# The first norm of four batches moved into the first cross attention, and first work of four stages issued one stage early

## The chip, the cores and the metric

One core of a Trainium2 chip runs the whole program. The metric is the device time of one execution in microseconds (us). TensorE multiplies, VectorE (DVE), ScalarE (ACT) and GpSimd (POOL) do the rest, and SyncE (SP) starts the transfers. "PE" is TensorE in the rows below.

## The reference

`x` is 8 batches of 256 rows by 256 columns; `ctx` is 8 batches of 64 rows. Four sublayers follow each other, each on a layernorm of `x`:

```python
x = x + tanh(g_xattn[0]) * cross_attention_0(layernorm(x), ctx)   # 16 heads of 128, 4 key heads, norm of q and k
x = x + tanh(g_ffn[0])   * block_0(layernorm(x))                   # h = x + causal self attention(layernorm(x)); h + mixture of 4 experts(layernorm(h))
x = x + tanh(g_xattn[1]) * cross_attention_1(layernorm(x), ctx)   # rotary, keys = context keys and own causal keys
x = x + tanh(g_ffn[1])   * feed_forward_1(layernorm(x))            # silu(gate) * up, down, 704 wide
```

All is float32. Matmuls that need it are done as three matmuls of split values (high by high, low by high, high by low).

## The kernel before

The residual `R` stays on the chip for all 8 batches, and so do `XTh` and `XTl`, the transposed normalised input of the current stage in a high and a low part. The program is six stages one after the other: the opening `c0` (context keys and values, first norm of all 8 batches, splitting of the first weights), the first cross attention `x0`, the self attention `f0`, the experts `moe`, the second cross attention `x1`, and the feed forward `ff`. An attention stage has 32 steps: head group `g = i // 8`, batch `i % 8`. The experts have 32 steps too (batch `c // 4`, expert `c % 4`), and `ff` has 8 batches of 6 slices.

Within a stage each of the five engines has its own list of instructions, written out by hand in program order, and semaphores order them against each other. An engine works its list strictly in order: an instruction that waits holds back all behind it. At the end of a stage every engine drains, raises one semaphore `bar` (L117 in `phase_end`) and waits until all five have; POOL then clears the semaphores of the stage one by one (L121) before it goes on. Nothing of the next stage is issued before that: no transfer of its constants, no matmul.

The norm of a batch (`row_norm`) is a chain over four engines: `stats` on DVE (L174, L177), `inverse` on POOL (a small addition and a power, L182 and L184), `rows` on DVE (L189, both halves of the batch), `turn` on PE (four transposes, L197), then an ACT copy to `XTh` and a DVE subtraction to `XTl`.

In the opening these are ACT `high` (L413) and DVE `low` (L458), done for b = 0 to 7 in a loop; POOL's list has `norm.inverse(b)` and `weights(b)` (L145, L147) in turn, and SP's list has the eight weight transfers, each behind `split_done`, and behind them six small ones (L334 to L336), the last of which it awaits.

A step of `x0` is on DVE a softmax (`softmax`, L802 to L824) with `queries` for two steps ahead (L795); on ACT the exponential (L733), the copy of the transposed queries (`q_ev`, L717), `squares` (L728) and the copy of the transposed probabilities (L771); on POOL `low_w` and `norms` (L585, L588), which waits for `squares(i + 2, s, 1)`; on PE projections `proj(i + 2)` (L285 to L287), `q_tr` (L639), `scores` (L650), `p_tr` (L660), `out_proj` (L671), and every second step `vw` (into `pO`).

`f0` begins with seven transfers of constants (L923 to L928), then the projections 0 to 5 of step 0. Its queries and keys are rotated in chains: PE projection, ACT `swapped` (L1097), POOL three operations of 128x512 (L1388, L1391, L1394), DVE `take` (L1240). `moe` begins with the gates on DVE and ACT, with `up(0)` to `up(2)` on PE and ten transfers on SP, the spilled rows `moe_xs` (awaited by DVE in `bias(0)`, L2222) last but one. `x1` begins with the projections of step 0, their rotation and norm on DVE, ACT and POOL, and their transposes, before `scores(0, 0)` (L1532, L1534) and the first `soft` (L1784). Its end norms batches 6 and 7 after the last outputs are added. `ff` begins with three transfers of constants; ACT and DVE wait for all three (`const`, 48).

Of the kernel before, what the change touches and what calls it, by code (L numbers as in the profile page):

```python
# [24 lines left out]
P = 128  # L25
B, S, D = 8, 256, 256
SC = 64
# [41 lines left out]
def build(nc, d, out, spill, stop=99):  # L69
    ctx = ExitStack()  # L70
    with ctx:
# [89 lines left out]
        be1 = sb("be1", [P, E * D // P])  # L161
        before = sb("before", [P, E, E])

        def row_norm(name, scope, xn=None):
# [7 lines left out]
            def stats(e, b):  # L172
                for t in range(T):
                    e.bn_stats(bst[:, b % 2, t, :], R[:, T * b + t, :]).then_inc(s_bs, 1)  # L174
                e.wait_ge(s_bs, T * b + T)
# [4 lines left out]
            def inverse(e, b):  # L180
                e.wait_ge(s_st, b + 1)
                e.tensor_scalar(rstd[:, 0, b, :], mv[:, 0, b, :, 1], 1e-5, 1.0, ALU.add, ALU.mult).then_inc(s_p, 1)  # L182
                e.wait_ge(s_p, b + 1)
                e.tensor_tensor(rstd[:, 0, b, :], rstd[:, 0, b, :], mhalf[:, 0:T], ALU.pow).then_inc(s_rs, 1)  # L184

            def rows(e, b):
                e.wait_ge(s_rs, b + 1)
# [5 lines left out]
            def turn(e, b, bank):  # L193
                e.wait_ge(s_xn, b + 1)
# [103 lines left out]
        def first_stage(name, q, norm, cT, wkv, kb, sq, ss, KT, VT, bq, bk, bv, wcol, mask):  # L298
# [42 lines left out]
            def pe(e):  # L341
# [41 lines left out]
                for b in range(3, B):  # L383
                    norm_tr(b)
                phase_end(e, name)

            def act(e):
# [50 lines left out]
                for b in range(3, B):  # L438
                    high(b)
                phase_end(e, name)  # L440

            def dve(e):
# [27 lines left out]
                for b in range(B):  # L470
                    if b + 2 < B:
                        stats(b + 2)
                    low(b)
                    if b + 2 < B:
                        rows(b + 2)
                e.wait_ge(q["late"], 32)
# [3 lines left out]
            def pool(e):  # L480
# [24 lines left out]
            return Phase(sp, pool, act, dve, pe)  # L505

        x0 = ExitStack()

        def cross_attention_0():
# [36 lines left out]
            names = ("raw0", "raw1", "hi", "split", "proj", "qb", "sq", "rqa", "rq", "tr", "te",  # L546
# [6 lines left out]
            def sp(e):  # L553
                def body(i, s, nxt):
                    if nxt:
# [15 lines left out]
            def pool(e):  # L571
# [18 lines left out]
                def body(i, s, nxt):  # L590
# [21 lines left out]
            def pe(e):  # L612
                def proj(i, s, t):
                    e.wait_ge(q["split"], pos(i - 3))
                    slot = (i // 8) % 2
# [7 lines left out]
                def vw(i, hp):  # L623
# [55 lines left out]

                def body(i, s, nxt):  # L680
# [9 lines left out]
                    if i in (29, 31):  # L690
                        turn(i, i - 29)
                    if s == 0:
# [9 lines left out]
                    if not last:  # L702
                        scores(i + 1)
                    p_tr(i)
                    if i in (29, 31):
                        turn(i, i - 28)
                    if not first:
                        out_proj(i - 1, 1 - s)
                in_order(e, NI, body, 24)
# [1910 lines left out]
```

## Time and profile before

| | |
|---|---|
| median of 3 runs | 1831.43 us (1830.64 to 1831.76) |
| the profiled execution | 1833.69 us, span 1831.9 us |
| PE busy | 1717.3 us, 94% of the span |
| DVE, ACT, POOL busy | 61%, 72%, 58% |
| DMA | 40.69 MB, 22 GB/s |
| mean granted clock of PE | 0.975 |

The span is the time from the first to the last instruction of the profiled execution; the time of a run holds some 2 us more. In the page's 40 slices PE stands at 9 tenths nearly everywhere; the slices at the stage seams are the ones that don't: slice 1 (5), slice 8 (7 and 8 around 340 us) and slices 21, 24 and 37 to 39. The stages run from about 0 to 45.6 us (opening), to 335 (`x0`), to 953 (`f0`), to 1092 (`moe`), to 1711 (`x1`), and to the end (`ff`).

### The profile page before, as it was taken

To read this page: it belongs to the slowest core of one execution; us is meant where nothing else is said; L and a number is where in the kernel's file an instruction comes from. 1 tells how busy PE (TensorE), PEld (TensorE's weight loads), DVE (VectorE), ACT (ScalarE), POOL (GpSimd) and SP (SyncE) were. 2 spreads that over 40 slices of the span, in tenths; PEclk is the share of its full clock that TensorE was granted. 3 is DMA by queue.
4 is the path that set the end of the run, shared out by engine and by line. 5 is a ranking of instruction groups with operands and counts; after the bars stand their busy time and mean duration, and the time that the engine had idled before them with its cause. 6 is when DMAs were issued, how large, how long until landed. Compare 5 with 4: busy or idle time off the path is not lost.

```text
span 1831.9 us, 36545 instructions
## 1 busy us (share of the span) xinstructions
PE 1717.3 (94%) x11584; PEld 1559.8 (85%) x11584; DVE 1118.2 (61%) x3129; ACT 1327.2 (72%) x4300; POOL 1064.2 (58%) x1208
## 2 busy tenths in 40 slices
PE   5999999799999999999989978999999999998798
PEld 3788888588999999999977867888888888888797
DVE  5577778477766666666867774555555555565222
ACT  4677777588888888888855627888888888888211
POOL 4333337699989889899823115444444444454454
PEclk8999999899999999999989989999999999999899
DMA  4000001100000000000011100000000000000000
GB/s 135 18 16 18 16 30 53 53 19 13 18 19 19 18 19 13 19 13 19 13 59 43 29 18 5 12 9 12 9 12 9 12 9 18 14 21 8 9 19 24
DMA packets 29533, 40.69 MB, mean 22 GB/s; under 512 B 4896, under 2 KB 18464, under 8 KB 29216
## 3 DMA queue, kind: packets, MB, share of 16 engines
q1 hardware_dynamic: 29344, 38.35, 6.9%
q8 instruction: 97, 1.59, 0.4%
q14 instruction: 92, 0.75, 0.1%
HBM read 34.14 MB, written 4.19 MB: 21 GB/s over the span
## 4 chain that ended last, share of the span: by engine, by line
PE 65%; ACT 14%; issue 6%; POOL 5%; DVE 4%; DMA 1%; SPq 0%; POOLq 0%; ACTq 0%; DVEq 0%
PE pS L978 4%; PE pF L285 4%; ACT pA L1642 4%; PE pF L287 4%; PE pF L286 4%; PE pA L287 4%; PE pA L285 4%; PE pA L286 3%; PE pA L969 3%; PE pF L671 3%; PE pA L971 3%; PE pA L970 3%; PE pS L650 3%; PE pO L997 3%; ACT x_P L1668 3%
## 5 line engine op out<-in xcount | busy, mean ns | idle before, releaser
L285 PE MATMUL pA<-Wh,XTh 128*128 128x512 f32 (+1 forms) x512 | 221.8, 433 | 5.2 <-DVEq L117 2.9
L1388 POOL TENSOR_TENSOR f_sw<-f_sw,f_sin 128x512 f32<-128x512 f32 x128 | 181.4, 1417 | 44.2 <-ACT f_sw L1097 44.2
L287 PE MATMUL pA<-Wh,XTl 128*128 128x512 f32 (+1 forms) x512 | 189.0, 369 | 0.0
L286 PE MATMUL pA<-Wl,XTh 128*128 128x512 f32 (+1 forms) x512 | 188.0, 367 | 0.0
L1097 ACT ACTIVATE f_sw<-pA 64x512 f32<-64x512 f32 x256 | 151.7, 593 | 35.4 <-PE pA L971 31.5
L1391 POOL TENSOR_TENSOR f_sw<-f_sw,f_RB 128x512 f32<-128x512 f32 x128 | 169.2, 1322 | 10.0
L969 PE MATMUL pA<-XTh,Wh 128*128 128x256 f32 x512 | 163.4, 319 | 8.1 <-DMA wg<-in_w_gate 7.2
L1668 ACT ACTIVATE x_P<-x_P,x_nm 128x192 f32<-128x192 f32 (+1 forms) x256 | 127.9, 505 | 35.8 <-DVE x_nm L1784 35.8
L280 POOL TENSOR_TENSOR Wl<-RAW,Wh 128x256 fp32r<-128x256 f32 (+3 forms) x64 | 60.7, 949 | 155.3 <-ACT Wh L273 155.3
L970 PE MATMUL pA<-XTl,Wh 128*128 128x256 f32 x512 | 145.2, 284 | 0.0
L971 PE MATMUL pA<-XTh,Wl 128*128 128x256 f32 x512 | 145.2, 284 | 0.0
L1895 POOL TENSOR_TENSOR x_QR<-x_QR,x_t 128x512 f32<-128x512 f32 x64 | 82.3, 1286 | 99.9 <-DVE x_QR L1761 99.9
L1118 ACT ACTIVATE f_P<-f_P,f_nm 128x128 f32<-128x128 f32 (+1 forms) x256 | 114.0, 447 | 22.5 <-DVE f_nm L1257 22.2
L1676 ACT ACTIVATE x_P<-x_P,x_rs 128x192 f32<-128x192 f32 (+1 forms) x256 | 116.2, 507 | 7.2 <-DVE x_rs L1792 7.2
L285 PEld LDWEIGHTS pA<-Wh,XTh 128*128 128x128 f32 x512 | 97.9, 191 | 26.3 <-DVEq L117 3.7
L1784 DVE CUSTOM_DVE_ANT_0 x_P<-pS,x_mask,x_nrq 128x192 f32<-128x192 f32 (+1 forms) x256 | 113.3, 480 | 4.5 <-PE pS L1534 3.7
L286 PEld LDWEIGHTS pA<-Wl,XTh 128*128 128x128 f32 x512 | 98.0, 191 | 18.7
L287 PEld LDWEIGHTS pA<-Wh,XTl 128*128 128x128 f32 x512 | 97.5, 191 | 17.3
L978 PE MATMUL pS<-f_kT,f_qT 128*128 128x128 f32 (+1 forms) x512 | 106.2, 330 | 5.7 <-POOL f_kT L1394 5.7
L1257 DVE CUSTOM_DVE_ANT_0 f_P<-pS,f_mask 128x128 f32<-128x128 f32 (+1 forms) x256 | 80.8, 353 | 48.9 <-PE pS L978 47.9
L969 PEld LDWEIGHTS pA<-XTh,Wh 128*128 128x128 f32 x512 | 98.3, 192 | 11.4 <-issue 7.5
L1126 ACT ACTIVATE f_P<-f_P,f_rs 128x128 f32<-128x128 f32 (+1 forms) x256 | 101.6, 448 | 3.1 <-DVE f_rs L1265 3.0
(286 smaller groups left out, 6093.4 us busy)
## 6 DMA issues: line engine op xcount, KB each, us to landing
RAW<-in_w_f SPq DMA_DIRECT2D x32, 256.0 KB, 2.7
RAW<-in_w_x SPq DMA_DIRECT2D x32, 160.0 KB, 2.2
RAW<-in_w_x SPq DMA_DIRECT2D x32, 128.0 KB, 2.1
RAW<-in_w_ff SPq DMA_DIRECT2D x8, 288.0 KB, 2.7
R<-in_x SPq DMA_DIRECT2D x4, 512.0 KB, 7.2
x_spill<-R SPq DMA_DIRECT2D x8, 256.0 KB, 2.0
RAW<-in_w_moe SPq DMA_DIRECT2D x8, 256.0 KB, 2.6
moe_xs<-x_spill SPq DMA_DIRECT2D x8, 256.0 KB, 3.0
```

Source lines behind the costliest of these rows:

```text
L285: e.matmul(o, ah, bh, start=first, stop=False)
L286: e.matmul(o, ah, bl, start=False, stop=False)
L287: return e.matmul(o, al, bh, start=False, stop=last)
L969: e.matmul(o, Wh[g % 2][:, w], xh, start=(k == 0), stop=False)
L970: e.matmul(o, Wh[g % 2][:, w], xl, start=False, stop=False)
L971: ins = e.matmul(o, Wl[g % 2][:, w], xh, start=False, stop=(k == KD - 1))
L978: ins = e.matmul(pS[:, h % 2, OFF[t]:OFF[t] + WID[t]], qT[:, i % 2, h, t * P:(t + 1) * P], kT[:, i % 2, h, 0:WID[t]], start=True, stop=True)
L1097: ins = e.activation(sw[dst, n, :, :], pA[src, n % 2, :].rearrange("p (a n) -> p a n", a=2), ACT.Copy)
L1388: e.tensor_tensor(y, y, bc(sind[:, :], 1, 2), ALU.mult).then_inc(q["swm"], 1)
L1391: e.tensor_tensor(y, y, RB[:, g % 2, 2 * n:2 * n + 2, :], ALU.add).then_inc(q["swb"], 1)
L1668: ins = e.activation(x, x, ACT.Exp, scale=-1.0, bias=nm[:, h, t:t + 1], accum_out=sm[:, h, t:t + 1])
L1676: ins = e.activation(x, x, ACT.Copy, scale=rs[:, h, t:t + 1])
```

## The change

Six things change; what is computed stays the same.

1. Opening: `norm` is done for batches 0 to 3 only. POOL still splits all eight weight pieces.
2. `x0`, steps 0 to 3: the norm of batches 4 to 7 (`late`). In steps 0 and 2 two batches get `stats` and `rows` on DVE and `inverse` on POOL; in steps 1 and 3 they are turned into `pO`, copied by ACT and subtracted by DVE.
3. Seam `x0` to `f0`: `f0`'s constants are loaded in step 20 of `x0`; its projections 0 and 1 are done by PE in and after the last step.
4. Seam `f0` to `moe`: `up(0)` and `up(1)` (12 matmuls of 256 columns each) are done in the last step of `f0`.
5. Seam `moe` to `x1`: the head of `x1` up to the transposes of step 0 and the keys and values of step 1 is laid into and behind the last four steps of `moe`, on all engines. Some tiles of `moe` share memory with tiles of `x1`.
6. Seam `x1` to `ff`: `ff_gs` and `ff_us` are loaded in `x1`, the table of Silu is loaded at its end, the first two slices of `ff` are projected in its last step. The norm of batches 6 and 7 moves into the first two batches of `ff`.

```diff
@@ opening
-                for b in range(3, B):
-                    norm_tr(b)
+                norm_tr(3)
@@ opening, pool
-                for b in range(2, B):
-                    norm.inverse(e, b)
-                    weights(b)
+                for c in range(2, 8):
+                    if c < 4:
+                        norm.inverse(e, c)
+                    weights(c)
@@ x0, sp
+                    if i == 20:
+                        self_constants(e)
@@ x0, pool: body, behind norms(i + 2, s)
+                    if i in (0, 2):
+                        late.inverse(e, i + 4)
+                        late.inverse(e, i + 5)
@@ x0, pe
+                    if t == 0 and 4 <= i < B:
+                        e.wait_ge(q["llo"], i - 3)
...
+                    if i in (2, 4) and hp == 0:
+                        e.wait_ge(q["llo"], i)
...
+                    if i in (1, 3):
+                        late_turn(i, i + 3)
                     if s == 0:
                         vw(i, 0)
...
                     if not last:
                         scores(i + 1)
+                    else:
+                        next_proj(0)
                     p_tr(i)
...
+                    if i in (1, 3):
+                        late_turn(i, i + 4)
                     if not first:
                         out_proj(i - 1, 1 - s)
...
                 in_order(e, NI, body, 24)
+                next_proj(1)
                 out_proj(NI - 1, (NI - 1) % 2)
@@ x0, act: behind squares(i + 2, s, 0), and again behind squares(i + 2, s, 1) with i + 4
+                    if i in (1, 3):
+                        late_high(i + 3)
@@ x0, dve: softmax
                     if two_more:
                         queries(i + 2, s, 0)
+                    if i in (1, 3):
+                        late_low(i + 3)
                     e.wait_ge(q["ex"], i + 1)
@@ x0, dve: body
                     if two_more:
                         queries(i + 2, s, 1)
+                    if i in (0, 2):
+                        late.stats(e, i + 4)
+                        late.stats(e, i + 5)
+                        late_rows(i + 4)
+                        late_rows(i + 5)
+                    if i in (1, 3):
+                        late_low(i + 4)
@@ f0, pe: last step
                     if one:
                         proj(j, 4)
+                    else:
+                        next_up(0)
...
                     if one:
                         scores(j, 0)
+                    else:
+                        next_up(1)
@@ moe, pe: behind down(c)
+                    if c == NU - 4:
+                        e.wait_ge(q["split"], B)
+                        e.wait_ge(q["nlo"], 2)
+                        head.proj_kv(e, 0)
+                    if c == NU - 3:
+                        head.proj_q(e, 0, 0)
+                    if c == NU - 2:
+                        head.proj_q(e, 0, 1)
+                head.proj_kv(e, 1)
+                head.q_tr(e, 0, 0)
+                head.q_tr(e, 0, 1)
                 norm_tr(B - 1)
+                head.k_tr(e, 0)
@@ moe, dve
+                    if c == NU - 2:
+                        head.rotate_k(e, 0)
+                    if c == NU - 1:
+                        head.take_q(e, 0, 0)
...
                 norm_stats(B - 1)
+                head.take_q(e, 0, 1)
                 norm_rows(B - 1)
+                head.rotate_k(e, 1)
                 norm_low(B - 1)
@@ moe, pool
+                head.sum_q(e, 0, 0)
                 norm.inverse(e, B - 1)
+                head.sum_q(e, 0, 1)
+                head.inverse_norms_q(e, 0)
+                head.inverse_norm_k(e, 1)
+                head.sum_k(e, 1)
@@ x1, pe: last step, behind scores(i, 2), and next_up(e, 1) behind p_tr(i, 2)
+                    if not one:
+                        next_up(e, 0)
@@ x1, pe: end
                 out_proj(NI - 1, 0)
-                norm_tr(6)
                 out_proj(NI - 1, 1)
-                norm_tr(7)
@@ ff, dve
+                        if i == 0 and m == 1:
+                            scale_result()
+                        if i == 0 and m in (2, 3):
+                            norm.stats(e, 4 + m)
+                        if i == 0 and m in (4, 5):
+                            norm.rows(e, 2 + m)
```

## Rows read from the trace of the kernel before

**Rows 1.** The page, the chain that ended last: shares of the span by engine.

```profile
PE 65%; ACT 14%; issue 6%; POOL 5%; DVE 4%; DMA 1%; SPq 0%; POOLq 0%; ACTq 0%; DVEq 0%
```

**Rows 2.** Windows: length, busy time (x instructions) of PE, PEld, DVE, ACT, POOL, clock.

```profile
95.00:300.00 205.00, 204.23 (x1270) 181.99 (x1269) 160.51 (x287) 159.52 (x621) 82.79 (x116) 1.00 0.08 24
1716.00:1800.00 84.00, 80.27 (x663) 79.04 (x662) 21.26 (x43) 18.53 (x39) 48.53 (x81) 1.00 0.05 17
```

**Rows 3.** Timeline, end of the opening: start, length, instruction [idle before, releaser].

```profile
30.98 0.71 POOL L184 TENSOR_TENSOR rstd<-rstd,mhalf 128x2 f32<-128x2 f32 x1
31.80 1.20 DVE L189 TENSOR_SCALAR n_xn<-R,mv,rstd 128x256 f32<-128x256 f32 x2 [0.60 <-POOL rstd L184]
...
41.74 1.20 DVE L189 TENSOR_SCALAR n_xn<-R,mv,rstd 128x256 f32<-128x256 f32 x2 [0.59 <-POOL rstd L184]
...
45.63 0.79 PE L285 MATMUL pA<-Wh,XTh 128*128 128x512 f32 x1 [1.46 <-DVEq L117]
```

**Rows 4.** Timeline and DMA view, the opening's weights and last transfers.

```profile
21.48 15.04 SPq L136 DMA_DIRECT2D RAW<-in_w_x  x6
38.93 0.43 SPq L336 DMA_DIRECT2D before<-in_earlier  x1
...
before<-in_earlier SPq DMA_DIRECT2D x1, 8.0 KB, 2.6
...
28.80 0.73 POOL L147 TENSOR_TENSOR Wl<-RAW,Wh 128x256 fp32r<-128x256 f32 x1
```

**Rows 5.** Timeline of DVE, POOL and ACT, steps 0 to 3 of `x0`.

```profile
64.55 0.68 DVE L795 TENSOR_TENSOR x_qb<-pA,x_bq 128x512 f32<-128x512 f32 x1
66.69 0.69 DVE L802 TENSOR_TENSOR x_P<-pS,x_rq 128x512 f32<-128x512 f32 x1 [1.46 <-PE pS L660]
...
84.50 0.69 DVE L802 TENSOR_TENSOR x_P<-pS,x_rq 128x512 f32<-128x512 f32 x1 [1.58 <-PE pS L660]
...
68.86 1.66 POOL L588 TENSOR_TENSOR x_rq<-x_rq,mhalf 128x8 f32<-128x8 f32 x1
...
69.66 0.63 ACT L733 ACTIVATE x_P<-x_P 128x512 f32<-128x512 f32 x1 [0.91 <-DVE x_P L813]
70.20 1.07 ACT L717 ACTIVATE x_qT<-pT 128x512 f32<-128x512 f32 x2
```

**Rows 6.** The chain in order of time: squares, and `out_proj` at either clock.

```profile
282.33 1.27 ACT x_sq L728 x8
...
299.30 1.73 PE pF L671 x8
...
318.79 3.43 PE pF L671 x8
```

**Rows 7.** Timeline, end of `x0` and start of `f0`.

```profile
334.42 0.25 DVE L214 BATCH_NORM_AGGREGATE mv<-bst 128x2 f32<-128x6 f32 x2
...
339.98 0.55 PE L969 MATMUL pA<-XTh,Wh 128*128 128x256 f32 x1 [7.17 <-DMA wg<-in_w_gate]
...
344.26 1.27 POOL L1388 TENSOR_TENSOR f_sw<-f_sw,f_sin 128x512 f32<-128x512 f32 x1 [11.94 <-ACT f_sw L1097]
```

**Rows 8.** Timeline of DVE, start of `moe`.

```profile
965.07 1.35 DVE L2222 SCALAR_TENSOR_TENSOR moe_xs<-moe_b,moe_gcomb,moe_xs 128x256 f32<-128x256 f32 x2 [3.48 <-DMA moe_xs<-x_spill]
```

**Rows 9.** Timeline, end of `moe` and start of `x1`.

```profile
1091.22 0.69 DVE L2242 TENSOR_TENSOR XTl<-pF,XTh 128x512 fp32r<-128x512 f32 x1 [1.90 <-ACT XTh L2122]
...
1101.33 1.28 POOL L1895 TENSOR_TENSOR x_QR<-x_QR,x_t 128x512 f32<-128x512 f32 x1 [0.58 <-DVE x_QR L1761]
...
1107.41 0.41 DVE L1784 CUSTOM_DVE_ANT_0 x_P<-pS,x_mask,x_nrq 128x192 f32<-128x192 f32 x1
...
1117.41 0.70 PE L1552 MATMUL pO<-x_PT,x_V 128*128 128x256 f32 x2 [2.88 <-POOL x_VS L1872]
```

**Rows 10.** Timeline, end of `x1` and first slices of `ff`.

```profile
1710.08 1.26 POOL L1914 TENSOR_TENSOR XTl<-x_KT,XTh 128x512 fp32r<-128x512 f32 x1 [2.70 <-ACT XTh L1697]
...
1717.73 0.39 PE L2360 MATMUL pA<-XTh,Wh 128*128 128x256 f32 x1 [1.48 <-DVE ff_h L2413]
```

More of the change, by code:

```diff
@@ L437, in act @@
                 take_keys(3)
-                for b in range(3, B):
-                    high(b)
+                high(3)
                 phase_end(e, name)
@@ L796, in queries, with late_rows, late_low @@
                                     ).then_inc(q["qb"], 1)
+                def late_rows(b):
+                    e.wait_ge(q["ltr"], pos(b - 5))
+                    late.rows(e, b)
+                def late_low(b):
+                    e.wait_ge(q["lhi"], b - 3)
+                    e.tensor_tensor(XTl[:, :, columns(b)], pO[:, :].rearrange("p (k n) -> p k n", k=KD),
+                                    XTh[:, :, columns(b)].bitcast(F32), ALU.subtract).then_inc(q["llo"], 1)
                 def softmax(i, s, two_more):
@@ L1033, in pe, with next_up @@
                 e.wait_ge(q["const"], 96)
-                for n in range(NQ):
+                def next_up(c):
+                    e.wait_ge(q["taken"], NQ * NI)
+                    e.wait_ge(q["split"], NI - 6)
+                    e.wait_ge(q["nlo"], 1)
+                    experts_up(e, c)
+                for n in range(2, NQ):
                     proj(0, n)
@@ L1415, in cross_attention_1, with cross_head @@
+        Head = namedtuple("Head", "q QR qT kT V KR nrq at_p at_qk place proj_kv proj_q q_tr k_tr take_kv squares q_ev k_ev "
+                          "take_q rotate_k context_keys inverse_norm_k sum_k sum_q inverse_norms_q t2")
+        def cross_head(scope, KT, tables):
             cosT, sinT, cosk, sink = tables
             NU, NT = 3, 3
[L1417 to L1421 removed]
@@ L1474, in table, with proj_kv @@
                 return bc(halves(x[:, t, :]), 1, HG)
+            def proj_kv(e, i):
+                g = i // 8
+                if g:
+                    e.wait_ge(q["split"], 8 * (g - 1) + 5)
+                e.wait_ge(q["tq"], pos(T * (i - 1) + 1))
+                for t in range(T):
+                    for k in range(KD):
+                        cc = slice(WKV + k * 2 * HD, WKV + (k + 1) * 2 * HD)
+                        ins = three(e, pA[:, NU * i % 2, t * 2 * HD:(t + 1) * 2 * HD], x_part(XTh, i, k, t),
+                                    x_part(XTl, i, k, t), Wh[(g + 1) % 2][:, cc], Wl[(g + 1) % 2][:, cc],
+                                    k == 0, k == KD - 1)
+                ins.then_inc(q["proj"], 1)
@@ new lines, in proj_q @@
+            def proj_q(e, i, t):
+                g = i // 8
+                if g:
+                    e.wait_ge(q["split"], 8 * (g - 1) + 4)
+                if t == 0:
+                    e.wait_ge(q["tq"], T * i)
+                else:
+                    e.wait_ge(q["tk"], i + 1)
+                for k in range(KD):
+                    cc = slice(k * GW, (k + 1) * GW)
+                    ins = three(e, pA[:, (NU * i + 1 + t) % 2, :], x_part(XTh, i, k, t), x_part(XTl, i, k, t),
+                                Wh[(g + 1) % 2][:, cc], Wl[(g + 1) % 2][:, cc], k == 0, k == KD - 1)
+                ins.then_inc(q["proj"], 1)
@@ new lines, in take_kv, with squares @@
+            def take_kv(e, i):
+                e.wait_ge(q["proj"], NU * i + 1)
+                e.wait_ge(q["pv"], pos(HG * (i - 2)))
+                x = pA[:, NU * i % 2, :].rearrange("p (t a n) -> p t a n", t=T, a=2)
+                for t in range(T):
+                    e.activation(sk[:, t, :], x[:, t, 0, :], ACT.Square, accum_out=ssk[:, t:t + 1])
+                e.activation(V[:, i % 3, :, :], x[:, :, 1, :], ACT.Copy).then_inc(q["kv"], 1)
+            def squares(e, i, t):
+                e.wait_ge(q["rot"], T * i + t + 1)
+                e.wait_ge(q["rqa"], i)
+                for h in range(HG):
+                    x = pA[:, (NU * i + 1 + t) % 2, h * HD:(h + 1) * HD]
+                    ins = e.activation(x, x, ACT.Square, accum_out=ssq[:, t, h:h + 1])
+                ins.then_inc(q["tq"], 1)
@@ L1841, in dve @@
                     if two:
[L1842 removed]
+                        take_q(e, k, 0)
                     if one:
@@ L2435, in body @@
                                         ALU.subtract).then_inc(q["hl"], 1)
+                        if i == 0 and m in (3, 4):
+                            norm.inverse(e, 3 + m)
                         if m == 4 and not (i == 0):
```

623 lines of the change are left out of this document (315 added, 308 removed).

## The prediction

> **What bounds the kernel now.** I read first the chain of waits on the page: it runs through PE for 65% of the span [rows 1]. The windows come next: in `x0` from 95 to 300 us PE is busy 204.23 of 205 us at full clock, and in `ff` 80.27 of 84 us [rows 2]. So inside those stages only PE time counts, and time can come only from where PE is not fed. These places are the seams, and the timelines around them give the terms. The reader is to see there which engine starts last: at each seam something small (a norm, a transfer, a power on POOL) is waited for by everything, because all five engines meet.
>
> **The change part by part.**
>
> **Opening, shorter.** The norm of one batch takes the loop from one L189 to the next: from 31.80 (batch 4) to 41.74 (batch 7) there are four, 3.31 us apart [rows 3]. Four batches less would be 13.3 us, but SP and POOL don't drop any work. SP's six weight transfers now start over 15.04 us, from 21.48 [rows 4]; they wait for POOL's splits, which wait in the list for the norms. Freed from batches 4 on, two buffers, a transfer of some 2 us and a split of some 1.2 us (its second half is 0.73 [rows 4]) give a piece each 1.8 to 2 us, so that the last starts at about 33.3 us instead of some 36. Behind it stand the six small ones; the last, now issued at 38.93, lands 2.6 us after its issue [rows 4]. It would be issued at 36 and land at 38.6. `x0` begins now at 45.63 [rows 3] and then at 38.7: a gain of 6.9 us. Bounds: 13.3 (if SP is not late) and 5.
>
> **Steps 0 to 3 of `x0`, longer.** This is the large unknown. In step 0 DVE is done with `queries` at 65.2 and starts the softmax of step 1 at 66.69 [rows 5]. Between them now stand `stats` for two batches and `late_rows(4)`, which waits for POOL. POOL's `late.inverse` is listed behind `norms(2)`, whose power runs from 68.86 to 70.52 [rows 5]; that itself waits for ACT's squares in step 0, and is not held up by DVE. An inverse is an addition and a power of 0.71 [rows 3], about 0.95 with the gaps: the two end at 71.5 and 72.4. So `rows(5)` ends at 73.2, and the softmax of step 1 starts 6.6 us late. PE stands too: its step 1 now begins with `late_turn(4)`, which waits for `rows(4)` at 72.3. The same engines that would cover it stand behind it: queued behind DVE's wait are softmax and queries, behind PE's the projections, `q_tr` and scores.
>
> Then `late_low(4)` stands ahead of the sum of the exponentials. It waits for ACT's `late_high(4)`, listed behind exponential 0.63, query copies 1.07 [rows 5] and squares 1.27 [rows 6]; with the copy of 0.6 and the subtraction of 0.7 the sum begins some 4.3 us after the softmax's subtraction instead of 0.7: 3.6 more. Followed on to step 2, which waits for `late_low(5)` behind ACT's second squares, `vw(2, 0)` starts 8.6 to 9 us late. Steps 2 and 3 do the same again with batches 6 and 7: the softmax of step 3, now at 84.50 [rows 5], starts at 99.7, its `late_low(6)` costs 3.6 again, and step 4 starts on PE 18.9 us late. Afterwards PE has no slack to recover anything [rows 2]. I add 0.5 for the lower clock at restarts: 19.4 us. Lower bound: only the work itself on PE, 4 x 4 transposes, some 2 us. Upper bound: 19.4 and the time of one step more, 28. I take 19.4, since every wait in it has its row.
>
> Opening and steps together: 12.5 us slower.
>
> **Seam `x0` to `f0`.** DVE ends at 334.67; then come the constants, and PE starts at 339.98, released by the transfer of `wg`; POOL's first rotation starts at 344.26 after ACT's copy [rows 7]. From there POOL's chain of 1.3 us operations sets the pace for some 70 us, so its start is the measure. With projections 0 and 1 done, ACT needs 2.1 us from the seam (bias 0.9, copy 1.2), and POOL itself clears semaphores for about 2.6. It starts at 334.7 + 2.6 = 337.3: 7.0 earlier. Cost: `next_proj(0)` fits a gap of 2.5 us in PE in the last step, `next_proj(1)` is 1.4 to 2.6 us ahead of the last output projection, whose wait for DVE covers about one; on the other side more work there may bring the clock back, which cuts 1.7 from an output projection (3.43 against 1.73 [rows 6]). I take 0.3. Gain 6.7, bounds 5 and 9. The transfers in step 20 go into a wait of SP and cost nothing; without that cover it would be 3 us once.
>
> **Seam `f0` to `moe`.** The first slices don't decide: DVE waits 3.48 us for `moe_xs` until 965.07 [rows 8], SP issues as many transfers as before, and ACT's first gelu waits for the gates. `up(0)`, 12 matmuls of 0.12 (80.27 us for 663 [rows 2]), falls into a gap; `up(1)` has 1.4 us and a gap of 0.6. Nothing gained and 0.9 lost; bounds -1 and +2.5.
>
> **Seam `moe` to `x1`.** Now DVE ends at 1091.91, the first `soft` is at 1107.41 and the first `attend` at 1117.41, released by POOL [rows 9]. In the tail DVE gets `rotate_k(0)` and `take_q(0, 0)` ahead of the last `combine` (0.9 late), and behind the norm's statistics there is a chain: `take_q(0, 1)` 1.2, POOL's sum 1.28 [rows 9], the power of eight 1.66 (the same form as in [rows 5]) with its two neighbours 2.3, the key norm 1.0, `rotate_k(1)` 1.1, sum 0.7. It ends at 1096.3 instead of 1091.9. From the seam on, scores, `soft`, two projections at the lower clock, their rotation, squares, the power and the context values (1.2) take 13.4 us: `attend(0, 0)` at 1109.7. Gain 7.7; bounds 6 and 9.5.
>
> **Seam `x1` to `ff`.** The two slices go into a stretch where PE has no gap: 2 x 1.43, so the last outputs come 2.85 us later. Two norm chains behind them fall away: the seam moves from 1711.34 to about 1705.6. `up(2)` on PE, now at 1717.73 [rows 10], needs only Silu (0.45) and one DVE operation after the seam: 1707.15, 10.6 earlier. Against this up to 2.2 for two slices at the lower clock (I take 1.8), 0.9 for eight transposes and 0.5 for `rows(7)`, which waits for POOL. Gain 7.4, bounds 5.5 and 9.
>
> **Sum.** -6.9 + 19.4 - 6.7 + 0.9 - 7.7 - 7.4 = -8.4 us. The span is 1831.9, the profiled execution 1833.69, its run being 2.3 over the median of 1831.43; the sum goes against the median: 1823.0 us.
>
> **The clock.** At 299.30 eight matmuls of `out_proj` take 1.73 us, at 318.79, behind gaps, 3.43 [rows 6]: the clock fell from 2.4 to 1.2 GHz after PE had stood. The Trainium skill (TensorE: Matmul & The Clock Gate, Why this matters for your kernels) advises against idle gaps between bursts of matmuls, since a long one brings the slow clock back. By it the new stalls of 6 us in steps 0 and 2 cost more than their length; by the row above the same could follow, and this is rival C.
>
> **The rivals.** A is the forecast, 1823: 0.55, from 1819 to 1827.
>
> B: the late norms stay hidden. For: DVE (161 of 205 us) and POOL (83) have room [rows 2]. Against: the lists are strict, and `late_rows` stands behind a power that ends at 70.5. If POOL's and ACT's order hurt half as much, steps 0 to 3 cost 7 to 9: 1811 to 1813. Chance 0.12.
>
> C, slower: the stalls leave PE at 1.2 GHz beyond step 3. A pair of steps is 16.5 us of PE work at full clock (205 us hold 25 steps [rows 2]), so a step at half clock takes some 8 us more where PE alone bounds it. In steps 1 to 3, which take 14 us each by my sum, that is hidden; in steps 4 and 5 it is not: 16 us more, 1839. It decides from 8.4 us on, which is one such step. Against: behind the present stalls of the stage's start the clock is 1.00 from 95 us on [rows 2], and `ff` holds it through short gaps. Chance 0.10.
>
> D: a seam's gain is given back, since another engine is late behind it (POOL's clearing in `x1`, the moved norm in `ff`, SP in the opening). A quarter of the 21.8 us of the last three gains (6.7, 7.7, 7.4) lost is 5.4: 1828.4. Chance 0.20. The remaining 0.03: the opening gains all 13.3, 1817.
>
> **How the numbers follow.** What can be told from no change is about 0.2%, 3.7 us. Faster (under 1827.8): A, B, the rest, and a quarter of D: 0.74. Same: most of D and a little of C, 0.17. Slower: C, 0.09. The range leaves out most of C and the end of B: 1813 to 1831.
>
> **What would show it.** `x0` starts near 38.7. DVE has a wait of some 4 us for POOL before L189 in step 0 and again in step 2, and one for ACT before the subtraction; PE stands 6 us before four transposes. 200 us later `x0` is 12 us behind. POOL's first rotation comes 2.6 us after the last DVE instruction of `x0`. In `moe` the wait for `moe_xs` stays. `x1` starts with scores. If PE has no stall before those transposes, or `x0` ends earlier than before, the largest term is wrong.

## The result

The changed kernel takes 1821.17 us (median of 5, 1818.29 to 1821.95) where the kernel before takes 1831.43: ratio 0.9942, 95% interval 0.9927 to 0.9957. In a second timing, beside the last experiments, it took 1823.09 us (median of 6) and the ratio was 0.9941. So it is 10.6 us faster (7.9 to 13.4 by the interval), and the forecast was 8.4. One execution of the kernel before in that second set took 4073 us; the ratios leave it out. The profiled execution took 1818.29 us with a span of 1816.5, the fastest of the five. Against the profiled execution of before its span is 15.4 us shorter; some 5 us of this are the choice of executions (see the last section), so sums over both traces are read with that in mind.

### The profile page after: what moved, and what is told of

It reads as the page before. It is cut to its first block, busy times and chain, and to the rows that moved or that the text cites. A ratio compares the mean times of both kernels' runs of the same rounds, so it can differ in the third digit from the quotient of the medians.

```text
span 1816.5 us, 36524 instructions
## 1 busy us (share of the span) xinstructions
PE 1709.1 (94%) x11584; PEld 1556.2 (86%) x11584; DVE 1116.9 (61%) x3131; ACT 1324.4 (73%) x4299; POOL 1062.6 (58%) x1206
## 4 chain that ended last, share of the span: by engine, by line
PE 65%; ACT 15%; issue 6%; POOL 6%; DVE 5%; DMA 1%; SPq 0%; POOLq 0%; ACTq 0%; DVEq 0%
PE pS L1064 4%; PE pF L290 4%; PE pF L292 4%; PE pF L291 4%; ACT pA L1628 4%; PE pA L292 4%; PE pA L290 4%; PE pA L291 3%; PE pA L538 3%; PE pA L539 3%; PE pA L540 3%; PE pO L1083 3%; PE pS L713 3%; ACT x_P L1850 3%; ACT x_P L1858 2%
## 5 line engine op out<-in xcount | busy, mean ns | idle before, releaser
L1947 DVE TENSOR_TENSOR x_OTl<-pO,x_OTh 128x256 fp32r<-128x256 f32 x128 | 54.3, 424 | 82.3 <-ACT x_OTh L1864 78.8
```

## The profile after

The chain of waits is made of the same parts as before [rows 1]:

```profile
PE 65%; ACT 15%; issue 6%; POOL 6%; DVE 5%; DMA 1%; SPq 0%; POOLq 0%; ACTq 0%; DVEq 0%
```

The windows of the changed kernel (columns as in [rows 2]). The steps with the moved norms, 63 to 110 us, are no stretch of full PE any more: 36.43 us busy of 47, at a mean clock of 0.87. The rest of `x0` is as full as before.

```profile
63.00:110.00 47.00, 36.43 (x196) 31.11 (x196) 31.14 (x62) 23.48 (x89) 13.02 (x21) 0.87 0.04 12
110.00:300.00 190.00, 190.00 (x1181) 169.33 (x1181) 146.88 (x260) 146.88 (x578) 71.61 (x96) 1.00 0.10 27
```

**Opening and steps 0 to 3 of `x0`.** Timeline of PE in the changed kernel. The first line is the start of `x0`, 45.63 before [rows 3]: 8.28 us sooner. The second and fourth are `late_turn(4)` and `late_turn(6)` behind their waits for DVE's rows; the third and fifth are `vw(2, 0)` and `vw(4, 0)` behind `late_low`.

```profile
37.35 0.80 PE L290 MATMUL pA<-Wh,XTh 128*128 128x512 f32 x1 [7.28 <-SPq L117]
...
64.18 1.09 PE L202 MATMUL pO<-ident,x_xn 128*128 128x128 f32 x4 [6.00 <-DVE x_xn L194]
...
77.71 0.47 PE L290 MATMUL pO<-Wh,x_VSh 128*128 128x512 f32 x1 [0.98 <-DVE XTl L895]
...
91.07 1.08 PE L202 MATMUL pO<-ident,x_xn 128*128 128x128 f32 x4 [4.20 <-DVE x_xn L194]
...
104.59 0.47 PE L290 MATMUL pO<-Wh,x_VSh 128*128 128x512 f32 x1 [0.98 <-DVE XTl L895]
```

Timeline of DVE: in steps 0 and 2 `late_rows` waits for POOL's power, and in steps 1 and 3 each of the four `late_low` waits for ACT. The first and last lines are the softmax of steps 0 and 5.

```profile
50.98 0.69 DVE L902 TENSOR_TENSOR x_P<-pS,x_rq 128x512 f32<-128x512 f32 x1 [5.38 <-POOL x_rq L644]
...
63.30 0.73 DVE L194 TENSOR_SCALAR x_xn<-R,mv,rstd 128x256 f32<-128x256 f32 x2 [4.58 <-POOL rstd L189]
...
71.60 0.69 DVE L895 TENSOR_TENSOR XTl<-pO,XTh 128x512 fp32r<-128x512 f32 x1 [2.71 <-ACT XTh L866]
...
76.87 0.69 DVE L895 TENSOR_TENSOR XTl<-pO,XTh 128x512 fp32r<-128x512 f32 x1 [2.42 <-ACT XTh L866]
...
90.19 0.74 DVE L194 TENSOR_SCALAR x_xn<-R,mv,rstd 128x256 f32<-128x256 f32 x2 [4.50 <-POOL rstd L189]
...
98.49 0.69 DVE L895 TENSOR_TENSOR XTl<-pO,XTh 128x512 fp32r<-128x512 f32 x1 [2.06 <-ACT XTh L866]
...
103.76 0.69 DVE L895 TENSOR_TENSOR XTl<-pO,XTh 128x512 fp32r<-128x512 f32 x1 [2.42 <-ACT XTh L866]
...
112.17 0.69 DVE L902 TENSOR_TENSOR x_P<-pS,x_rq 128x512 f32<-128x512 f32 x1 [1.47 <-PE pS L723]
```

The same two softmaxes in the kernel before:

```profile
59.35 0.69 DVE L802 TENSOR_TENSOR x_P<-pS,x_rq 128x512 f32<-128x512 f32 x1 [5.39 <-POOL x_rq L588]
...
100.95 0.69 DVE L802 TENSOR_TENSOR x_P<-pS,x_rq 128x512 f32<-128x512 f32 x1 [1.58 <-PE pS L660]
```

The five steps between them took 41.60 us and now take 61.19: 19.6 more. With the start 8.28 sooner, `x0` is 11.3 late.

**`x0` to `f0`.** Timelines of DVE, ACT and POOL in the changed kernel, for [rows 7]. DVE's last instruction of `x0` ends at 343.55, POOL's first rotation starts 3.05 us later. Before, it was 9.59 us from the end at 334.67 to 344.26: 6.5 less.

```profile
343.30 0.25 DVE L219 BATCH_NORM_AGGREGATE mv<-bst 128x2 f32<-128x6 f32 x2
...
343.63 0.91 ACT L1202 ACTIVATE f_RB<-f_sin,f_bqk 128x256 f32<-128x256 f32 x2 [5.05 <-DVEq L117]
344.56 1.19 ACT L1194 ACTIVATE f_sw<-pA 64x512 f32<-64x512 f32 x2
345.66 0.89 ACT L1202 ACTIVATE f_RB<-f_sin,f_bqk 128x256 f32<-128x256 f32 x2
...
346.60 1.27 POOL L1485 TENSOR_TENSOR f_sw<-f_sw,f_sin 128x512 f32<-128x512 f32 x1 [3.58 <-ACT f_RB L1202]
```

The row names ACT's second pair of biases as the releaser, because they ended last before 346.60. But the rotation waits only for ACT's copy (`q["sw"]` in its code), and in the kernel before and in e5 and e9 it starts 0.14 us after the end of that copy. Here the copy ends at 345.75, 2.20 us after DVE's last instruction, and POOL starts 0.85 us later still, so something of POOL's own holds it back. Between `bar` and that wait its list has only the clearing of `x0`'s semaphores and the wait for the constants, which have long landed; so it is the clearing. The seven kernels that have the late norms, early constants and early projections all show 3.05 or 3.06 us. In e1, whose `x0` has eight semaphores fewer to clear (three of its own and the five of the late norm), it is 2.48 us behind the same copy at 2.20. Timelines of DVE and POOL of e1:

```profile
332.27 0.25 DVE L219 BATCH_NORM_AGGREGATE mv<-bst 128x2 f32<-128x6 f32 x2
...
335.00 1.27 POOL L1459 TENSOR_TENSOR f_sw<-f_sw,f_sin 128x512 f32<-128x512 f32 x1 [3.38 <-ACT f_sw L1168]
```

Inside `f0` the delay falls from 2.3 us at the first rotation to 0.3 at the second attended head of the last step. Of this 1.3 us come at once, at the 25th rotation (2.6 us late one rotation earlier, 1.3 from here on). Timelines of POOL, before and changed:

```profile
453.59 1.30 POOL L1388 TENSOR_TENSOR f_sw<-f_sw,f_sin 128x512 f32<-128x512 f32 x1 [2.10 <-ACT f_sw L1097]
```

```profile
454.89 1.29 POOL L1485 TENSOR_TENSOR f_sw<-f_sw,f_sin 128x512 f32<-128x512 f32 x1 [0.70 <-ACT f_sw L1194]
```

The two projections that PE has fewer to do are not the reason: e6 and e7 have them early as well and show no such fall, and e11, which does them all in `f0`, falls by 2.5 us there. What causes it stays open.

**`f0` to `moe`.** The two early products cost 0.6 us in the last step of `f0`. Timelines of DVE, the second and the last head of that step, before and changed; 0.32 us late become 0.89:

```profile
932.04 0.43 DVE L1269 TENSOR_TENSOR f_OTl<-pO,f_OTh 128x256 fp32r<-128x256 f32 x1 [1.11 <-ACT f_OTh L1132]
...
939.39 0.42 DVE L1269 TENSOR_TENSOR f_OTl<-pO,f_OTh 128x256 fp32r<-128x256 f32 x1 [0.85 <-ACT f_OTh L1132]
```

```profile
932.36 0.42 DVE L1366 TENSOR_TENSOR f_OTl<-pO,f_OTh 128x256 fp32r<-128x256 f32 x1 [1.10 <-ACT f_OTh L1229]
...
940.28 0.42 DVE L1366 TENSOR_TENSOR f_OTl<-pO,f_OTh 128x256 fp32r<-128x256 f32 x1 [0.85 <-ACT f_OTh L1229]
```

DVE's first wait in `moe`, 3.48 us until 965.07 before [rows 8], stands, and ends 0.55 us later:

```profile
965.62 1.36 DVE L2333 SCALAR_TENSOR_TENSOR moe_xs<-moe_b,moe_gcomb,moe_xs 128x256 f32<-128x256 f32 x2 [3.18 <-DMA moe_xs<-x_spill]
```

By the middle of `moe` the changed kernel is 0.7 us ahead, so this stage's start gave some 1.6, and the seam 1.0 net of the cost ahead of it.

**`moe` to `x1`.** For [rows 9]: the first scores, for which PE waits until POOL, the last engine of `moe`, has raised `bar`, and the first `attend` (1117.41 before), which is 8.25 us sooner: 7.5 for the seam.

```profile
1095.71 1.01 PE L1740 MATMUL pS<-x_kT,x_qT 128*128 128x192 f32 x2 [4.10 <-POOLq L117]
...
1109.16 0.84 PE L1760 MATMUL pO<-x_PT,x_V 128*128 128x256 f32 x2 [2.87 <-POOL x_VS L2015]
```

**`x1` to `ff`.** For [rows 10]: the last accumulation that ends `x1`, and `up(2)`, 1717.73 before. It is 17.4 sooner, of which 7.2 were there in the middle of `x1`. From the second batch on 8.3 of the 10.2 are left.

```profile
1698.29 0.75 DVE L1954 SCALAR_TENSOR_TENSOR R<-pF,tanhg,R 128x512 f32<-128x512 f32 x1 [3.23 <-PE pF L292]
...
1700.31 0.36 PE L1517 MATMUL pA<-XTh,Wh 128*128 128x256 f32 x1 [2.06 <-DVE ff_h L2544]
```

## The experiments

Each time is given as its ratio to the kernel before in the same set of runs, since that one had medians of 1831.1, 1830.9 and 1834.4 us in the three sets. A ratio is known to 0.0009 to 0.0019, a difference of two to about 0.002, or 3.7 us; one step of 0.001 is 1.8 us. "Slower" and "faster" are against the changed kernel's 0.9942 unless another is named.

**e1. The late norms back in the opening, the seams as changed.** In the first stage and `x0`:

```
-                for b in range(4):          # DVE; PE, ACT and POOL alike
+                for b in range(B):
...
-                    if i in (1, 3):
-                        late_turn(i, i + 3)
```

> The changed kernel, but with the first norm of all 8 batches in the opening, as before; the work of the next stage at the four seams stays. Theory A (the late norms cost more than the shorter opening gives: between the two traces the first cross attention starts 8.3 us sooner and its fifth step's vw stands 11.3 us later): 11.3 us come off, 1810 us (1808 to 1812). Theory B (the late norms are hidden, the net delay of 11.3 us is made good later in the attention): 1820 to 1829, no faster than the changed kernel.

Measured: 1807.67 us (1806.75 to 1808.73), ratio 0.9873 (0.9859 to 0.9886): 0.0069 faster, 12.6 us. The five steps take 41.66 us again. Theory A holds, B falls.

**e2. The late norms alone, on the kernel before.** The same lines, added to it; no constant, projection or product moved.

> The kernel before with the late norms alone, nothing at the seams. Theory A: 1831.4 + 11.3 = 1842.7 us (1840 to 1845). Theory B: 1823 to 1832. If e1 and e2 are each 11 us off but on different sides of their base, the late norms and the seams add up; if e2 is less late than e1 is early, part of the late norms' cost is an effect of the two together.

Measured: 1838.81 us (1838.68 to 1844.04), ratio 1.0048 (1.0035 to 1.0062), 8.8 us slower. In its trace `x0` is 11.2 late from softmax 5 on and the end is 10.2 late (the profiled execution, 1844.04 us, was the slowest of the five). A again, though a little under its 1840 to 1845 us. That 8.8 is less than the 12.6 of e1 is inside the error of the two; the traces (11.2 here, 12.1 at the same softmax between e1 and the changed kernel) leave at most 0.9 us for an interplay.

**e3. Statistics and rows where DVE waits anyway.** At the start of `x0`:

```
                    if first:
+                        for b in range(4, B):
+                            late.stats(e, b)
                         for k in (0, 1):
                             queries(k, k, 0)
                             queries(k, k, 1)
+                        late_rows(4)
+                        late_rows(5)
...
-                    if i in (0, 2):
-                        late.stats(e, i + 4)
-                        late.stats(e, i + 5)
-                        late_rows(i + 4)
-                        late_rows(i + 5)
+                    if i == 2:
+                        late_rows(6)
+                        late_rows(7)
```

and on POOL the four `late.inverse` ahead of `vs(0)`.

> The changed kernel with the statistics of batches 4 to 7 ahead of the attention's first work on VectorE, their inverses first on GpSimd, and the rows of batches 4 and 5 ahead of the first softmax; the rows of 6 and 7 stay at the end of step 2, now without a wait for GpSimd. Theory A1 (what delays steps 0 to 3 is VectorE's queue: 9.4 us of waits for GpSimd, 4.0 us of statistics and 1.7 us of rows leave the steps): 13 to 15 us faster than the changed kernel, some 1807 us. Theory A2 (the delay is the handovers TensorE to ScalarE to VectorE of the turned blocks, the waits of 2.1 to 2.7 us for XTh): only the rows that came off the front count, some 4 to 6 us, 1816 us.

Measured: 1807.91 us (1807.02 to 1810.02), ratio 0.9876 (0.9862 to 0.9889): 12.1 us faster. Timeline of DVE: the waits for POOL are gone, those for ACT stand as they were, and softmax 0 to softmax 5 takes 48.56 us.

```profile
50.31 0.69 DVE L901 TENSOR_TENSOR x_P<-pS,x_rq 128x512 f32<-128x512 f32 x1 [4.09 <-issue]
...
63.90 0.69 DVE L894 TENSOR_TENSOR XTl<-pO,XTh 128x512 fp32r<-128x512 f32 x1 [2.71 <-ACT XTh L865]
...
69.16 0.69 DVE L894 TENSOR_TENSOR XTl<-pO,XTh 128x512 fp32r<-128x512 f32 x1 [2.42 <-ACT XTh L865]
...
98.87 0.69 DVE L901 TENSOR_TENSOR x_P<-pS,x_rq 128x512 f32<-128x512 f32 x1 [1.58 <-PE pS L722]
```

The first softmax stands 13.6 us after the start of `x0` in both, so nothing was paid ahead of the steps. So 12.6 of the 19.6 us were the statistics, the rows and DVE's waits for POOL between them; A1 named the cause, and its 13 to 15 was a little high. The other 7.0 stay.

**e4. And the low halves behind the softmax.** Both pieces leave their old places, ahead of the sum of the exponentials and behind the second squares.

```
                     ... ALU.mult).then_inc(q["pn"], 1)      # end of softmax(i)
+                    if i in (1, 3):
+                        late_low(i + 3)
...
+                    if i in (1, 3):                         # ACT
+                        late_high(i + 4)
                     if not (i >= NI - 2):
                         squares(i + 2, s, 1)
```

> As e3, and in steps 1 and 3 the first low half stands behind the softmax instead of ahead of the sum of the exponentials, and the second block's high half stands ahead of the second squares on ScalarE. A1: the two waits of 2.7 and 2.1 us for XTh go too, but the second block of each step is turned later by the same handover: 1 to 3 us faster than e3, some 1805 us. A2: 4 to 5 us faster than e3, some 1811 us. Either way faster than both kernels.

Measured: 1801.85 us (1799.52 to 1804.6), ratio 0.9840 (0.9827 to 0.9853): 6.6 us faster than e3, and 18.7 faster than the changed kernel. By A1 it was to be 1 to 3 us, by A2 4 to 5; the time, known to 3.5 us, doesn't tell these apart. Timeline of DVE: the waits for ACT are 0.93 and 0.80 us, and softmax 0 to softmax 5 takes 41.53 us, as in the kernel before. The 7.0 us that e3 had left were the handovers that A2 named, so each theory was right about its part.

```profile
52.42 0.69 DVE L901 TENSOR_TENSOR x_P<-pS,x_rq 128x512 f32<-128x512 f32 x1 [4.09 <-issue]
...
66.00 0.69 DVE L894 TENSOR_TENSOR XTl<-pO,XTh 128x512 fp32r<-128x512 f32 x1 [0.93 <-ACT XTh L865]
...
68.08 0.69 DVE L894 TENSOR_TENSOR XTl<-pO,XTh 128x512 fp32r<-128x512 f32 x1 [0.80 <-ACT XTh L865]
...
93.95 0.69 DVE L901 TENSOR_TENSOR x_P<-pS,x_rq 128x512 f32<-128x512 f32 x1 [1.49 <-PE pS L722]
```

The late norms as such cost nothing in the five steps: all 19.6 us were the order in which they stood. (The first softmax stands 14.1 us after the start of `x0` instead of 13.6; in e11, with the same order, it is 13.6 again.) The two moves of e4 were not run one by one. Against e1, which has all norms in the opening, e4 is 0.0033 faster, 6.0 us: only in this order does the shorter opening pay.

**e5. The two early projections undone, the constants still early.**

```
-                    else:
-                        next_proj(0)
...
-                for n in range(2, NQ):
+                for n in range(NQ):
                     proj(0, n)
```

> The changed kernel, but the first two projections of the self attention are issued at its own start again; its constants still land early. Theory A (the gain of 9.1 us at this seam was the wait for the constants, 7.2 us on TensorE before): the phase ends at 343.8, the projections take the 4.3 us that they took before ahead of GpSimd's first rotation, 348.1 instead of 346.60: 1.5 to 2.5 us slower than the changed kernel, 1823 us. Theory B (the gain was the projections in the tail): 6 us slower or more, 1827 us.

Measured: 1819.85 us (1818.57 to 1823.1), ratio 0.9949 (0.9934 to 0.9964), 1.3 us slower or the same. B falls. Timelines of ACT and POOL: the first pair of biases takes ACT until 344.77 in any case, the projections run beside them, ACT's copy ends at 346.81, 0.8 us later than in the changed kernel, and the rotation starts 3.18 us after DVE's last instruction instead of 3.05. POOL's clearing hides the rest. At 819 us this kernel is 0.9 us behind the changed one; it had the same lateness until that one's fall at the 25th rotation, which doesn't go by the projections (see above).

```profile
343.86 0.91 ACT L1199 ACTIVATE f_RB<-f_sin,f_bqk 128x256 f32<-128x256 f32 x2 [4.81 <-DVEq L117]
345.61 1.20 ACT L1191 ACTIVATE f_sw<-pA 64x512 f32<-64x512 f32 x2 [0.85 <-PE pA L540]
...
346.95 1.27 POOL L1482 TENSOR_TENSOR f_sw<-f_sw,f_sin 128x512 f32<-128x512 f32 x1 [3.47 <-ACT f_sw L1191]
```

**e6. The experts' two early products undone.** `next_up(0)` and `next_up(1)` out of the last step of `f0`, `experts_up` for all of 0 to 2 at the start of `moe`.

> The changed kernel, but the experts' first two up products are issued at the stage's own start again. The forecast had them cost 0.9 us, so 0.9 us faster, 1820.3 us. By the traces the stage's combine of step 3 stands 1.2 us nearer in the changed kernel than the self attention's last step did, so rival B: 1 to 1.5 us slower, 1822.5 us. Rival C: the wait for moe_xs hides both, no difference within 0.5 us.

Measured: 1820.87 us (1818.2 to 1821.87), ratio 0.9948 (0.9935 to 0.9962). 0.0006 slower, 1.1 us: the time can't tell B, C and the forecast apart. In the trace this kernel falls back by 1.3 us against the changed one from the end of `f0` to the middle of `moe`, as B says; but it also saves the 0.6 us that the two products cost in the last step of `f0`, so that 0.7 us are left for them. DVE's first addition waits for the transfer here too, 3.21 us until 966.33.

**e7. The head of `x1` undone.** `head.proj_kv`, `proj_q`, `take_kv`, `take_q`, `rotate_k`, the sums and norms of steps 0 and 1 leave the tail of `moe` and stand at the start of `x1` in the order of before.

> The changed kernel, but the second cross attention's first projections, rotations and transposes stand at its own start again, as before. By the traces the seam gave 7.5 us (forecast 7.7): 1828.7 us (1827 to 1831). Rival (the gain is given back in the attention's first steps): under 4 us slower, 1825 us or less.

Measured: 1828.66 us (median of 12, 1824.81 to 1831.06), ratio 0.9992 (0.9981 to 1.0002): 9.2 us slower, by medians 7.5. Its first `attend` stands at 1117.36, where it was before, 8.2 us behind the changed kernel. Of these 1.2 are there before the seam, in the middle of `moe`; 7.0 are the head's. Nothing is given back in the steps that follow.

**e8. The seam to `ff` undone**, but for the scales and the table of Silu: the norms of 6 and 7 in the tail of `x1`, all slices in `ff`.

> The changed kernel, but the second cross attention's last two norms and the feed forward's first two up products stand where they stood before; the scales still land early and the table of Silu is still loaded at the tail. By the traces the seam gave 10.2 us at the third up product, of which 8.3 were left after the second batch (forecast 7.4). Theory A (norms and products): 6 to 8 us slower, 1828.2 us. Rival (most of it was the wait for the scales and the table load, 3.9 us after the phase's end): 3 to 4 us slower, 1825 us.

Measured: 1826.55 us (median of 12, 1823.99 to 1828.96), ratio 0.9981 (0.9972 to 0.9990): 7.1 us slower, by medians 5.4. A. Timeline of PE: the two norm chains are back, with the wait of 4.78 us ahead of the last transposes, which the kernel before has too, at 1708.00. From the last steps of `x1` to the end this kernel gains 1.1 us on the kernel before, where the changed one gains 8.3; so by this trace the early scales and table of Silu, which it keeps, are worth no more than 1.1.

```profile
1695.06 0.63 PE L202 MATMUL pT<-ident,x_KT 128*128 128x128 f32 x4 [1.24 <-DVE x_KT L194]
...
1701.90 1.08 PE L202 MATMUL pT<-ident,x_KT 128*128 128x128 f32 x4 [4.78 <-DVE x_KT L194]
```

**e9. The whole first seam undone**: e5, and `self_constants(e)` at the start of `f0`'s queue on SP.

> e5 with the self attention's constants loaded at its own start again, so the whole of this seam as before. Theory A (the seam's 9.1 us are the wait for the constants, since e5 lost nothing): 7 to 9 us slower than e5, 1828 us. Rival B (constants and products each hide the other: with either one early the other costs nothing): also slower, but under 5 us, 1824 us, because the rotation then waits for something that e5's trace shows too.

Measured: 1828.74 us (median of 12, 1825.53 to 1830.3), ratio 0.9971 (0.9961 to 0.9980). Against the changed kernel on the same chip (0.9941) 5.5 us slower, against e5 4.0. Timelines of SP, PE, ACT and POOL: six transfers are issued 0.47 us apart, `wg` last, at 345.73, and its landing frees PE and ACT. From DVE's end at 343.37 the rotation is 9.34 us away.

```profile
343.45 0.33 SPq L521 DMA_DIRECT2D f_cos<-in_cosd  x1
...
345.73 0.43 SPq L526 DMA_DIRECT2D wg<-in_w_gate  x1
```

```profile
348.44 0.55 PE L538 MATMUL pA<-XTh,Wh 128*128 128x256 f32 x1 [6.92 <-DMA wg<-in_w_gate]
...
351.37 1.20 ACT L1191 ACTIVATE f_sw<-pA 64x512 f32<-64x512 f32 x2 [2.05 <-PE pA L540]
...
352.71 1.27 POOL L1482 TENSOR_TENSOR f_sw<-f_sw,f_sin 128x512 f32<-128x512 f32 x1 [9.61 <-ACT f_sw L1191]
```

The cause is A, the constants. The size by the traces is 6.2 us (9.34 against 3.18), by the times 4.0, known to 3.3: under the 7 to 9 of A. The 9.1 that e5's and e9's expectations used was wrong as a measure of this seam: it also held some 2.5 us by which the last steps of `x0` were shorter than in the profile of before (there an output product in them took 3.29 us, here 2.5 us). Late constants with early products, the other half of B, were not run. In e9's trace the copy that releases POOL waits 2.05 us for PE after ACT's biases, so early products could have taken off some 2 us at most there, an estimate.

**e10. Only the two early slices of `ff` undone**, the norms still in `ff`.

> The changed kernel with the feed forward's first two up products at its own start; the two last norms stay in the feed forward. e8 undid both for 5.4 us. Theory A (the first product and what ScalarE, VectorE and GpSimd do with it are a chain at the phase's start: 1.4 us of product at either clock level up to 2.9): 3 to 5 us slower, 1825 us. Theory B (the tail's norm chain of 4.8 us on TensorE was the price): under 2 us slower, 1822.5 us.

Measured: 1820.40 us (1818.92 to 1822.55), ratio 0.9933 (0.9915 to 0.9950): not slower, by medians 2.7 faster than the changed kernel on the same chip, which its error doesn't tell from nothing. B. In its trace the accumulation of the last step but one in `x1` comes 2.8 us sooner for it, as long as the two slices take. From there to the end part of this is given back: counted from the last steps of `x1`, the end comes 1.1 us sooner than in the first profile of the changed kernel and 2.5 sooner than in the second (e12).

**e11. e4 without the parts that e5 and e6 showed to be worth nothing.**

> e4 without the early projections at the first seam and without the early up products at the second, which e5 and e6 showed to be worth nothing: 1801.9 us as e4 (1800 to 1804), since neither part has a price. Rival: with the attention 19 us sooner the constants arrive no earlier against the seam, and the projections are worth something after all: 1804 us or more.

Measured: 1805.23 us (1802.69 to 1806.58), ratio 0.9846 (0.9826 to 0.9865), 1.1 us over e4's ratio: the same within the error of 4 us. The 1805 us lie above the rival's 1804, but on a chip where the kernel before, too, took 1834.4 us and not 1831.1; so the ratio decides nothing for it. e4 has the lower figure and beats both kernels; e11 does it with less. e4 without the early slices of `ff` wasn't run.

**e12. The changed kernel again**, on the chip of e9 to e11.

> The changed kernel as it is, for a measure on the same chip as the others: 1821.2 us (1819 to 1823) by its first timing.

Measured: 1823.09 us (1820.72 to 1823.38), ratio 0.9941 (0.9926 to 0.9957).

## Why the prediction was right

The forecast for each term, what the two traces show, and what the undoing cost (us):

| term | forecast | traces | timed |
|---|---|---|---|
| opening | -6.9 | -8.3 | |
| steps 0 to 3 | +19.4 | +19.6 | |
| the two together | +12.5 | +11.3 | +12.6 (e1), +8.8 (e2) |
| `x0` to `f0` | -6.7 | -6.5 | -5.5 (e9) |
| `f0` to `moe` | +0.9 | -1.0 | -1.1 (e6) |
| `moe` to `x1` | -7.7 | -7.5 | -9.2 (e7) |
| `x1` to `ff` | -7.4 | -8.3 | -7.1 (e8) |
| elsewhere: end of `x0`, inside `f0`, inside `x1` | 0 | -2.4, -2.0, +1.0 | |
| sum | -8.4 | -15.4 | -10.6 (the result) |

A timed term is the difference of two ratios and known to 3 or 4 us. With e1 for the first two the timed terms add up to -10.3, near the result. The three parts of "elsewhere" belong to no change that was undone by itself: the end of `x0` and the inside of `f0` differ as much between executions (last section), and the loss inside `x1` is there in every kernel with the seams changed, 1.1 to 2.3 us, also in e7 and e8, and not in e2; its cause was not sought.

**Steps 0 to 3, the largest term, was right in its parts.** The waits came at the places named: DVE for POOL's power 4.58 and 4.50 us ahead of the rows ("some 4"), PE 6.00 us ahead of the four transposes ("6"), `late_low` behind ACT. `vw(2, 0)` stands 40.36 us after the start of `x0` and before 31.16, so 9.2 late for 8.6 to 9. Rival B (hidden norms) fell by e1. But e3 and e4 show what it was right about: the engines had room enough, and with another order in the same lists nothing of the 19.6 is left.

**Rival C** didn't come: the clock was 0.87 over 63 to 110 us and 1.00 from there on. The rule of the Trainium skill (TensorE: Matmul & The Clock Gate, Why this matters for your kernels) that idle gaps bring the slow clock back agrees with the 0.87; that steps 4 and 5 would pay for it no run shows.

**The opening** gained 1.4 more than forecast. The last pieces of the weights came 1.80 us apart on average (POOL begins to split the last four at 28.64 to 34.03), the lower end of the 1.8 to 2 that was taken, and SP issued its last small transfer at 34.71 instead of 36. It stayed well short of 13.3, for the reason given: SP.

**`x0` to `f0`: right in size and path, but the gain is not the products'.** ACT's copy was ready 2.20 us after the seam for the 2.1 forecast, and POOL's own clearing of semaphores set the start, 3.05 us for 2.6; that is why 6.5 us came off and not 7.0. The condition that the forecast put ahead of this, "With projections 0 and 1 done", carries almost nothing: without them the rotation starts 0.13 us later (e5). The gain is the transfers that no longer begin at the seam (e9, 6.2 us by the traces), and the forecast gave them no price. The row that had it was there: PE's wait for `wg` of 7.17 us in [rows 7].

**`f0` to `moe`** was forecast to cost 0.9. The wait for `moe_xs` stood, as forecast, and the loss came, 0.6 us in the last step of `f0`. But "Nothing gained" failed: some 1.6 us come back in the slices behind that wait, where the forecast stopped looking. Its sign was wrong by the traces (-1.0); the times, -1.1, don't settle it. **`moe` to `x1`** was right in its parts: POOL is the last engine and ends at 1095.59 (1096.3 forecast), and the first `attend` comes 13.6 us later (13.4). **`x1` to `ff`** was right in size: the ten kernels with the moved norms in `ff` give 5.5 to 9.6 us by the same reading, the most without the early slices (e10). The forecast charged the slices 2 x 1.43 us in the tail and credited them at the start; e10 shows that these two are all they do, and that the norms moved out of the tail carry the gain. **Rival D** (a gain given back) happened in part: of the 10.2 us at `up(2)` 1.9 were given back by the second batch, to the transposes and rows of the moved norms, inside what the forecast took off (3.2).

The forecast of -8.4 lies inside the interval of the result, so the 2.2 us between it and -10.6 need no cause. That it is so near is in part luck: terms of this size are known to 3 or 4 us each by the times, and two of the six had a reason or a sign that the runs did not bear out.

## What to carry to other kernels

Work that is moved from a start-up into a steady loop is priced by its place in each engine's list, not by its length: put each piece where that engine already waits and ahead of the other engine's long item, and here 19.6 us became 0. At a seam ask first which transfer is issued there: from `x0` to `f0`, starting it earlier was nearly the whole gain (6.2 of 6.5 us). Where no transfer is awaited, look for the chain over several engines, as the head of `x1` (7 us) and the last two norms (7 us); products issued early into a tail without a gap only changed sides. When the rest is gone, what is left at a seam can be the end of the stage itself: here POOL's clearing of semaphores, 3 us. Before a moved piece is kept, undo it alone: the early products at three of the four seams were worth 1.3 us or less each.

## What the runs showed that was not expected

**Two executions of one kernel differ at the seams.** The changed kernel's executions lay between 1818.29 and 1823.38 us, and the faster have the higher mean clock (0.98 against 0.977). Windows of the profiled one of the first timing (1818.29 us):

```profile
320.00:365.00 45.00, 34.63 (x201) 30.36 (x200) 27.16 (x69) 28.18 (x66) 38.25 (x52) 0.89 0.15 48
...
1080.00:1130.00 50.00, 36.51 (x206) 30.77 (x203) 27.27 (x80) 29.87 (x124) 23.54 (x35) 0.90 0.04 11
1130.00:1680.00 550.00, 540.17 (x3631) 487.18 (x3632) 306.68 (x1015) 460.57 (x1689) 268.86 (x367) 1.00 0.04 12
```

and of the second (1823.38 us):

```profile
320.00:365.00 45.00, 35.43 (x190) 31.03 (x189) 26.93 (x64) 26.91 (x65) 36.44 (x51) 0.85 0.14 48
...
1080.00:1130.00 50.00, 37.42 (x203) 31.66 (x203) 28.78 (x83) 28.00 (x114) 21.88 (x32) 0.86 0.04 11
1130.00:1680.00 550.00, 539.72 (x3633) 485.84 (x3632) 304.63 (x1006) 462.69 (x1695) 270.10 (x368) 1.00 0.04 12
```

The clock is lower in the second at both seams and the same between them; the same eight matmuls of an output product near the end of `x0` take 2.52 us in the first and 3.16 in the second. How well one trace gives a seam depends on the seam. From DVE's last instruction to the first rotation it is 3.05 or 3.06 us in every execution with the same edits there. But the last steps of `x0` are between 0.3 and 3.2 us shorter than before, `moe` to `x1` gives 7.3 to 8.1 us, and the delay at the 25th rotation falls by 1.2 to 2.5 us in five of the kernels and not at all in the others, with or without early projections. That is why the traces make the whole gain 15.4 and the times 10.6: the profiled execution of before lay 2.3 us over its median, that of the changed kernel 2.9 under its own. A part of the second execution's delay also grows slowly inside `x1` at a clock of 1.00 (2.5 us at the first `attend`, 3.6 at 1670); what that is stays open.

**Six transfers cost more by their issue than by the last one's bytes.** In e9 they stand some 0.47 us apart in SP's list, and the last, `wg` with 4 KB, lands 2.6 us after its issue; the four of 128 KB ahead of it take 2.0 to 2.7 us from issue to landing.
